# Causal attention of a two-layer model: values projected by pair of head groups instead of by batch element

## Chip, cores and metric

One core of one Trainium2 chip. The metric is the device time of one execution in microseconds; the program before takes 2349.78 us, the median of 3 runs (2348.75 to 2349.86).

## The reference, cut to what matters

Four batch elements of 1024 tokens with 512 channels go through a decoder layer (causal self-attention, cross-attention to 64 context rows, feed-forward) and then a gated fusion. The change touches the causal self-attention alone:

```python
xn1 = _ln(x, g1, be1)
q = einsum('btc,hcd->bhtd', xn1, Wq) + bq      # 16 heads of 32 channels
k = einsum('bsc,hcd->bhsd', xn1, Wk) + bk
v = einsum('bsc,hcd->bhsd', xn1, Wv) + bv
scores = einsum('bhtd,bhsd->bhts', q, k) / scale
scores = where(tril, scores, -inf)
out = einsum('bhts,bhsd->bhtd', softmax(scores), v)
```

## The kernel before

**The stages.** The program has a causal stage (the first 1000 us or so), a cross-attention stage and a feed-forward stage. The first steps of the cross stage (names that begin with "2") are planned into the end of the causal one.

**Groups.** The causal stage works through 16 groups, numbered g: group g is four heads of batch element b = g // 4. Each group has two halves of 512 query tokens (c2 = 0, 1). Half 0 meets 4 key tiles of 128 tokens, half 1 meets 8. For each key tile j and each head i of the group there is a score matmul (step "sc", L785), an exponential on ScalarE ("ex", L895; on diagonal tiles VectorE adds a mask first, "low", L1011), and a product with the values ("pv", L797): the 128x32 slice of the value tile for that head is the stationary operand, the exponentials move, and four heads fill the four column strips of bank 7. POOL adds up the exponentials (L660), and at the end of a half the step "fin" (L806) turns these sums into row sums on TensorE.

**Work for later groups, laid between.** While group g attends, TensorE also does, in the gaps of that order: the query and key projections of a group one or two ahead ("pj", four units for each group, lines 55 to 57), the row maxima of the next group ("mx", L745, reduced on VectorE by L1000 and L1004), the transposes of the next batch element's normalised input ("lnT", L722) in groups 1 and 2 of each batch element, and the value projections ("vm").

**Values before.** A unit of "vm" is one key tile: 128 tokens by all 512 value columns of one batch element, in one PSUM bank. Inputs and weights are split into a high and a low part, so each of the 4 channel tiles k takes three matmuls (the function three, lines 55 to 57): 12 matmuls of 512 moving columns a unit, 8 units for a batch element, 32 in all. ScalarE then copies the bank into Q.v ("ve", L873). Q.v is 128 x 8 x 512 and holds the values of one batch element, all key tiles. So the copy of key tile st for the next batch element has to wait until the last group of this one has used it in "pv". For that reason the eight units of batch element b stand in the last 69% of group 4b-1 and at the start of group 4b; for batch element 0 they stand ahead of group 0. At the very start Q.v also holds the raw input rows of batch element 0 (two of its eight slots for each quarter of the tokens), until they are transposed.

**What sets the order.** order1 gives every step a planned time; the unit is one group (group g runs from g to g + 1, half 1 begins at g + 0.31). at0 turns microseconds of the start-up into that unit: at0(72) is 0. All engines' programs and the queue of SyncE (SP), which issues the DMAs, go through the same list sorted by planned time, each taking its own steps in that order. The units of "vm", "pj" and "mx" are cut into small steps by spread, so that they stand between the score matmuls. banks1 hands the 7 other PSUM banks out ahead of time: each use takes the bank whose last use is planned to end first, and on the chip it waits until that last use has in fact been read. All waits are semaphores with counts known when the program is built.

Of the kernel before, what the change touches and what calls it, by code (L numbers as in the profile page):

```python
# [120 lines left out]

def order1():

    cut = 0.31
# [18 lines left out]
    for b in range(NB):  # L143
        for qt in range(4):
            if b:
                t += ln_times(b, qt, 4 * b - 2.5 if qt == 0 else 4 * b - 2.28 + 0.26 * qt, 4 * b - 2.05 + 0.25 * qt)
        for st in range(8):
            if b == 0:
                s, d = at0(44 + 3.1 * st), 0.05
            else:  # L150
                s, d = 4 * b - 1 + cut + (1 - cut) * (st + 2.2) / 9, 0.057
            t += spread(s, s + d, [(("vm", b, st, k), 1) for k in range(KT)])
            t.append((s + d, ("ve", b, st)))
    for g in range(16):
        if g == 0:
            at = [at0(a) for a in (25, 30, 35, 40)]
        elif g == 1:
            at = (-0.22, -0.13, -0.02, 0.08)
        elif g % 4 == 0:
            at = (g - 1.67, g - 1.5, g - 1.22, g - 1.11)  # L160
        else:
            at = (max(g - 1.87, 0.2), max(g - 1.63, 0.4), g - 1.4, g - 1.2)
        for c2 in range(2):
            for wq in range(2):
                n = 2 * c2 + wq
                t += proj_times(g, c2, wq, at[n], at[n] + (0.05 if g < 2 else 0.07 if g % 4 == 0 else 0.15))
                back = (g - 2 + cut, g - 2 + cut + (1 - cut) * 0.54, g - 1, g - 1)[n] + 0.03
                t.append((at[n] + 0.1 if g == 0 else max(at[n] + 0.22, back), ("stack", g, c2, wq)))
        m0, m1, end = (at0(46), at0(54), cut - 0.12) if g == 0 else (0.25, 0.5, 0.97) if g == 1 else (g - 1.02, g - 0.72, g)
        t += spread(m0, m1, max_steps(g, 0)) + spread(m1, end, max_steps(g, 1))  # L170
        for c2, at in enumerate((m1, end)):
            t += [(at + 0.04, ("mxT", g, c2)), (at + 0.06, ("tq", g, c2)), (at + 0.09, ("tqd", g, c2))]
        for c2 in range(2):
            steps = spread(g + cut * c2, g + (1 if c2 else cut), attn_steps(g, c2))
            t += steps
            for at, s in steps:
                if s[0] == "sc" and s[3] >= 4 * c2:
                    t += [(at + 0.014, ("low", *s[1:])), (at + 0.028, ("ex", *s[1:]))]
                elif s[0] == "sc":
                    t.append((at + 0.001, ("ex", *s[1:])))  # L180
            end = g + (1 if c2 else cut)
# [39 lines left out]

def order2():


    T, X0 = 0.207, 16.68
    E = X0 + 28 * T
    at2 = lambda n: X0 + T * n if n < 28 else E + 0.82 * T * (n - 28)
    t = [(a, s) for a, s in ((14.4, ("2kc",)), (14.66, ("2kb",)), (14.8, ("2wb",)), (14.87, ("2bw",)), (14.6, ("2z", 2)), (15.02, ("2z", 0)),
                             (15.03, ("2z", 1)), (14.9, ("2cd",)))]
    for k in range(KT):  # L230
        t += [(14.02 + 0.1 * k, ("2ld", 0, k)), (14.42 + 0.08 * k, ("2ld", 1, k)), (14.76 + 0.08 * k, ("2ld", 2, k)),
              (14.07 + 0.1 * k, ("2kv", 0, k)), (15.32 + 0.02 * k, ("2kv", 1, k))]
# [1924 lines left out]
```

## Time and profile before

| what | value |
|---|---|
| runs | 2349.86, 2348.75, 2349.78 us; median 2349.78 |
| span of the profiled execution, first to last instruction | 2338.9 us |
| what lies around it, against the median of the runs | 10.9 us |
| instructions | 31417 |
| mean granted TensorE clock | 0.976 |
| TensorE busy (matmuls) | 2198.0 us, 94% |
| VectorE, ScalarE, POOL busy | 60%, 37%, 40% |
| from the first score matmul of group 0 to that of group 14 | 113.3 to 898.7 us |

The profile shows one execution. The profiled execution's own time outside the profiler is not given; its span is 10.9 us below the median of the three runs, and differences are carried over from one to the other. A group's place in the trace is found by counting score matmuls (L785): there are 48 in each group, and the first of them is taken as the group's start. Matmuls are pipelined and the profile models their ends, so a matmul's own duration is longer than its share of the engine's time: what one costs in a run of them is the distance from start to start.

### The profile page before, as it was taken

The page shows a single profiled execution, that of the slowest core. Times are in us where ns is not written, and L with a number is a line of the kernel's source. Part 1 is how long each engine was busy: PE and PEld are TensorE (multiplying, and loading weights), DVE is VectorE, ACT ScalarE, POOL GpSimd, SP SyncE. Part 2 cuts the span into 40 slices and gives each one's busy share as a digit, 9 for nine tenths or more (in the row PEclk, how much of TensorE's full clock was granted, in tenths as well). Part 3 has the DMA queues.
Part 4 walks back from the last instruction along what each step waited for, and adds up shares of the span by engine and source line. Part 5 has one row for each costly group of instructions (what it writes and reads, how often), then busy time and mean ns, then how long its engine had stood idle before and what let it go on. Part 6 is the DMA issues. An engine that isn't in the chain of part 4 may idle for free.

```text
span 2338.9 us, 31417 instructions
## 1 busy us (share of the span) xinstructions
PE 2198.0 (94%) x11206; PEld 1595.5 (68%) x11206; DVE 1410.1 (60%) x3349; ACT 868.2 (37%) x1598; POOL 933.6 (40%) x943
## 2 busy tenths in 40 slices
PE   7999999999999998789999998999999999999996
PEld 5655565556555654447777776788887887888784
DVE  5477757875786566735666668453455546454646
ACT  3155545654565455533443334321111122112213
POOL 1068657766777577773333333010111202011212
PEclk9999999999999998789999999999999999999998
DMA  7465545553556356212111121321112121212011
GB/s 231 55 93 97 92 71 77 103 93 62 83 97 97 60 88 124 69 56 85 59 55 55 59 95 55 113 86 36 50 54 75 52 82 44 87 55 68 33 36 50
DMA packets 106320, 177.29 MB, mean 76 GB/s; under 512 B 18334, under 2 KB 23454, under 8 KB 106160
## 3 DMA queue, kind: packets, MB, share of 16 engines
q1 hardware_dynamic: 106164, 175.29, 32.4%
q8 instruction: 88, 1.44, 0.3%
q14 instruction: 68, 0.56, 0.1%
HBM read 83.67 MB, written 40.13 MB: 53 GB/s over the span
## 4 chain that ended last, share of the span: by engine, by line
PE 75%; DVE 9%; issue 6%; ACT 4%; POOL 3%; DMA 2%; SPq 0%; POOLq 0%; ACTq 0%; DVEq 0%
PE psum L55 18%; PE psum L56 17%; PE psum L57 17%; PE psum L797 5%; PE psum L745 5%; PE psum L785 4%; PE psum L806 2%; DMA small<-es 2%; PE psum L703 1%; DVE psum L1000 1%; POOL es L660 1%; ACT sx L1346 1%; PE psum L1300 1%; DVE mx L1004 1%; PE psum L1292 1%
## 5 line engine op out<-in xcount | busy, mean ns | idle before, releaser
L660 POOL TENSOR_TENSOR es<-es,er 128x512 f32<-128x512 f32 (+3 forms) x640 | 589.6, 961 | 322.5 <-PE psum L797 283.4
L895 ACT ACTIVATE er<-psum 128x512 f32<-128x512 f32 (+3 forms) x640 | 280.4, 470 | 316.0 <-DVE psum L1011 181.2
L1000 DVE CUSTOM_DVE_ANT_0 psum<-psum,mask_ts 128x384 f32<-128x384 f32 (+3 forms) x512 | 247.9, 500 | 201.2 <-PE psum L745 200.5
L785 PE MATMUL psum<-qs,ks 100*128 100x512 f32 (+3 forms) x768 | 264.5, 377 | 17.1 <-DVE mx L1004 6.6
L745 PE MATMUL psum<-ks,qs 96*128 96x512 f32 (+3 forms) x768 | 267.2, 373 | 10.9 <-DVE mx L1000 6.6
L1850 ACT ACTIVATE fy<-psum,cols 128x512 f32<-128x512 f32 x128 | 88.2, 689 | 451.4 <-PE psum L57 450.9
L745 PEld LDWEIGHTS psum<-ks,qs 96*128 96x128 f32 x768 | 144.0, 194 | 109.7 <-issue 39.4
L1004 DVE TENSOR_REDUCE mx<-psum 128x1 fp32r<-128x512 f32 x256 | 175.1, 684 | 60.7 <-PE psum L745 59.8
L785 PEld LDWEIGHTS psum<-qs,ks 100*128 100x128 f32 x768 | 145.9, 196 | 92.4 <-DVE mx L1004 23.1
L55 PE MATMUL psum<-fh,hh 128*128 128x512 f32 x512 | 201.1, 393 | 7.1 <-DVE hl L1951 7.1
L55 PE MATMUL psum<-fah,fh 128*128 128x512 f32 x512 | 202.6, 396 | 0.0
L57 PE MATMUL psum<-fah,fl 128*128 128x512 f32 x512 | 199.8, 390 | 0.0
L56 PE MATMUL psum<-fal,fh 128*128 128x512 f32 x512 | 199.6, 390 | 0.0
L57 PE MATMUL psum<-fh,hl 128*128 128x512 f32 x512 | 199.4, 389 | 0.0
L56 PE MATMUL psum<-fl,hh 128*128 128x512 f32 x512 | 199.3, 389 | 0.0
L1949 DVE CAST hh<-fy 128x512 fp32r<-128x512 f32 x128 | 59.5, 465 | 228.8 <-ACT fy L1850 228.4
L1215 POOL TENSOR_TENSOR pp<-pp,small 128x1024 f32<-128x1024 f32 x32 | 61.2, 1913 | 266.7 <-DVE small L1481 266.7
L797 PE MATMUL psum<-er,v 128*32 128x512 f32 (+3 forms) x1280 | 152.3, 497 | 6.7 <-ACT er L895 6.2
L1746 POOL TENSOR_TENSOR et<-et,vpb 128x512 f32<-128x512 f32 x24 | 35.4, 1476 | 284.8 <-ACT et L1876 284.8
L1011 DVE TENSOR_TENSOR psum<-psum,mask_st 128x128 f32<-128x128 f32 x512 | 138.3, 303 | 15.0 <-PE psum L785 14.1
L55 PEld LDWEIGHTS psum<-fh,hh 128*128 128x128 f32 x512 | 96.1, 188 | 29.0 <-DVE hl L1951 9.5
L57 PEld LDWEIGHTS psum<-fah,fl 128*128 128x128 f32 x512 | 96.2, 188 | 20.5
(258 smaller groups left out, 4479.8 us busy)
## 6 DMA issues: line engine op xcount, KB each, us to landing
qs<-stage SPq DMA_DIRECT2D x96, 256.0 KB, 5.7
ks<-stage SPq DMA_DIRECT2D x96, 256.0 KB, 6.9
rs<-rs_d SPq DMA_DIRECT2D x32, 256.0 KB
sa_d<-rs SPq DMA_DIRECT2D x32, 256.0 KB, 2.2
sx<-sa_d SPq DMA_DIRECT2D x8, 1024.0 KB, 5.7
xt<-in_x SPq DMA_DIRECT2D x32, 256.0 KB, 6.1
x_d<-xt SPq DMA_DIRECT2D x32, 256.0 KB, 2.0
fw<-in_Wf SPq DMA_DIRECT2D x16, 512.0 KB, 5.3
```

The lines of the kernel that those rows point to most:

```text
L55: e.matmul(dst, lh, rh, start=start, stop=False)
L56: e.matmul(dst, lh, rl, start=False, stop=False)
L57: return e.matmul(dst, ll, rh, start=False, stop=stop)
L660: e.tensor_tensor(es, es, er, ALU.add).then_inc(s_add.sem, 1)
L745: t = e.matmul(bank1(*s)[:, v * wd:v * wd + wd], Q.qs[par][0:96, i, 128 * ti:128 * ti + 128], Q.ks[par][0:96, i, c0:c0 + wd], start=True, ...
L785: t = e.matmul(ps[:, off:512], Q.ks[par][0:100, i, 128 * j:128 * j + 128], Q.qs[par][0:100, i, 512 * c2 + off:512 * c2 + 512], start=True, ...
L797: e.matmul(bank[BO][32 * i:32 * i + 32, off:512], Q.v[:, j, h:h + 32], src[:, off:512], start=j == 0, stop=j == nj - 1).then_inc(s_pv.sem, 1)
L895: e.activation(dst, bank1("sc", g, c2, j, i)[:, off:512], ACT.Exp, scale=SCALE).then_inc(s_freeS.sem, 1)
L1000: t = e.tensor_tensor_reduce(out=ps, in0=ps, in1=mask_ts[:, 512 - wd:512], scale=1.0, scalar=-3e38, op0=ALU.add, op1=ALU.max, accum_out=mx ...
L1004: e.tensor_reduce(mx[:, at:at + 1], bank1(*s)[:, 0:wd], AX, ALU.max).then_inc(s_red.sem, 1)
L1011: e.tensor_tensor(ps, ps, mask_st[:], ALU.add).then_inc(s_low.sem, 1)
L1850: e.activation(y[:], ring3(("h", c, m)), ACT.Relu, bias=col("bf1", m), scale=1.0).then_inc(s_r3.sem, 1)
```

## The change

Values are projected for a pair of groups (q = g // 2: eight heads, 256 columns) instead of for all sixteen heads of a batch element. A unit of "vm" is now two key tiles (sp: tiles 2sp and 2sp + 1) by 256 columns, the two key tiles in the two halves of one bank: 2 x 4 channel tiles x 3 matmuls, that is 24 matmuls of 256 moving columns. There are 4 units for a pair, 8 for a batch element, 32 in all. Q.v keeps its size; the pairs take its two halves in turn, and a pair's copy waits for the pair two before it. The planned times change with it: the units of pair q stand in 4 places from 1.4 or 1.2 groups ahead of the pair's first group. The other times become named constants with the same values, but for two small shifts: the projections of group 2 (0.13 and 0.37 instead of 0.2 and 0.4) and the restacking DMAs ("stack") of groups 4, 8 and 12 (at most 0.08 earlier).

```diff
+LN_LOAD = (-2.5, -2.02, -1.76, -1.5)
+LN_TURN = (-2.05, -1.8, -1.55, -1.3)
+CUT = (0.31, 0.31, 0.31, 0.31)
+PROJ_0 = (25, 30, 35, 40)
+PROJ_1 = (-1.22, -1.13, -1.02, -0.92)
+PROJ = ((-1.67, -1.5, -1.22, -1.11), (-1.87, -1.63, -1.4, -1.2), (-1.87, -1.63, -1.4, -1.2), (-1.87, -1.63, -1.4, -1.2))
+PROJ_LONG = (0.07, 0.15, 0.15, 0.15)
+VALUES_0 = (48, 54, 60, 66)
+VALUES = ((-1.2, -0.95, -0.7, -0.45), (-1.4, -1.1, -0.8, -0.5))
+VALUES_LONG = 0.1
 def order1():
-        for st in range(8):
-            if b == 0:
-                s, d = at0(44 + 3.1 * st), 0.05
-            else:
-                s, d = 4 * b - 1 + cut + (1 - cut) * (st + 2.2) / 9, 0.057
-            t += spread(s, s + d, [(("vm", b, st, k), 1) for k in range(KT)])
-            t.append((s + d, ("ve", b, st)))
     for g in range(16):
-            at = (max(g - 1.87, 0.2), max(g - 1.63, 0.4), g - 1.4, g - 1.2)
+        r = g % 4
+        at = [at0(a) for a in PROJ_0] if g == 0 else [g + a for a in (PROJ_1 if g == 1 else PROJ[r])]
-                t.append((at[n] + 0.1 if g == 0 else max(at[n] + 0.22, back), ("stack", g, c2, wq)))
+                t.append((at[n] + 0.1 if g == 0 else max(at[n] + PROJ_LONG[r] + 0.07, back), ("stack", g, c2, wq)))
+        if g % 2 == 0:
+            for sp in range(4):
+                s, d = (at0(VALUES_0[sp]), 0.05) if g == 0 else (g + VALUES[r // 2][sp], VALUES_LONG)
+                t += spread(s, s + d, [(("vm", g // 2, sp, i), 1) for i in range(4)])
+                t.append((s + d, ("ve", g // 2, sp)))
+        def values(g):
+
+            return Q.v[:, 4 * (g // 2 % 2):4 * (g // 2 % 2) + 4, :].rearrange("p a (s n) -> p (a s) n", n=256)
 def pe1(e, w):
                 elif s[0] == "vm":
-                    _, b, st, k = s
-                    if k == 0:
+                    _, q, sp, i = s
+                    b, half = divmod(q, 2)
+                    st = 2 * sp + i // 2
+                    if i == 0:
                         free1(w, *s[:3])
                     w.wait_ge(s_wl1, 12)
-                    xn_ready(w, b, st // 2, k)
-                    ss = slice(128 * st, 128 * st + 128)
+                    ss, cs, to = slice(128 * st, 128 * st + 128), slice(256 * half, 256 * half + 256), slice(256 * (i // 2), 256 * (i // 2) + 256)
                     Wh, Wl = Q.W["v"]
-                    t = three(e, bank1(*s[:3]), (Q.xh[:, k, ss], Q.xl[:, k, ss]), (Wh[:, k, :], Wl[:, k, :]), k == 0, k == 3)
-                    if k == 3:
+                    for k in range(2 * (i % 2), 2 * (i % 2) + 2):
+                        xn_ready(w, b, st // 2, k)
+                        t = three(e, bank1(*s[:3])[:, to], (Q.xh[:, k, ss], Q.xl[:, k, ss]), (Wh[:, k, cs], Wl[:, k, cs]), k == 0, k == 3)
+                    if i == 3:
                         t.then_inc(s_fillA.sem, 1)
...
-                        w.wait_ge(s_v, 8 * (g // 4) + j + 1)
+                        w.wait_ge(s_v, 4 * (g // 2) + j // 2 + 1)
...
-                        h = 128 * gg + 32 * i
-                        e.matmul(bank[BO][32 * i:32 * i + 32, off:512], Q.v[:, j, h:h + 32], src[:, off:512],
+                        h = 128 * (g % 2) + 32 * i
+                        e.matmul(bank[BO][32 * i:32 * i + 32, off:512], values(g)[:, j, h:h + 32], src[:, off:512],
 def act1(e, w):
                 elif s[0] == "ve":
-                    if b:
-                        w.wait_ge(s_pv, Q.pv[4 * b - 1, 1, st, 3] + 1)
-                    e.activation(Q.v[:, st, :], bank1("vm", b, st), ACT.Copy).then_inc(s_v.sem, 1)
+                    if q >= 2:
+                        w.wait_ge(s_pv, Q.pv[2 * q - 3, 1, 2 * sp + 1, 3] + 1)
+                    else:
+                        w.wait_ge(s_fillA, Q.useA["lnT", 0, 2 * q + sp // 2, 1] + 1)
+                    e.activation(values(2 * q)[:, 2 * sp:2 * sp + 2, :], bank1("vm", q, sp).rearrange("p (s n) -> p s n", n=256),
+                                 ACT.Copy).then_inc(s_v.sem, 1)
```

## Rows read from the trace of the kernel before

**Rows 1.** The page: span, busy time of TensorE, granted clock in 40 slices.

```profile
span 2338.9 us, 31417 instructions
...
PE 2198.0 (94%) x11206; PEld 1595.5 (68%) x11206; DVE 1410.1 (60%) x3349; ACT 868.2 (37%) x1598; POOL 933.6 (40%) x943
...
PEclk9999999999999998789999999999999999999998
```

**Rows 2.** Busy time by stretch, one stretch a group: window, width, engines' busy (instructions), clock.

```profile
72.00:113.30 41.30, 41.30 (x188) 29.31 (x188) 18.45 (x51) 7.13 (x13) 0.00 (x0) 1.00 0.17 23
113.30:167.50 54.20, 52.57 (x290) 32.62 (x288) 43.72 (x142) 27.62 (x58) 37.19 (x40) 1.00 0.62 91
167.50:218.80 51.30, 48.81 (x274) 28.61 (x273) 38.67 (x126) 28.90 (x61) 36.81 (x40) 0.97 0.55 83
218.80:276.70 57.90, 52.24 (x291) 30.91 (x289) 44.65 (x146) 35.32 (x71) 40.46 (x47) 0.97 0.53 102
276.70:344.00 67.30, 66.00 (x349) 43.29 (x348) 37.19 (x126) 31.05 (x65) 44.31 (x51) 1.00 0.48 77
344.00:394.10 50.10, 48.80 (x281) 29.78 (x277) 35.85 (x123) 28.14 (x60) 34.10 (x34) 1.00 0.47 70
394.10:446.10 52.00, 48.42 (x274) 28.68 (x273) 38.74 (x123) 29.04 (x61) 40.33 (x46) 1.00 0.59 93
446.10:503.10 57.00, 52.31 (x290) 30.92 (x288) 43.82 (x144) 35.28 (x71) 41.20 (x49) 0.97 0.54 104
...
620.50:673.90 53.40, 51.46 (x274) 30.73 (x273) 38.74 (x120) 28.93 (x61) 40.35 (x46) 0.90 0.58 91
673.90:731.40 57.50, 53.12 (x290) 31.08 (x288) 44.68 (x146) 35.28 (x71) 41.10 (x48) 0.94 0.54 103
...
848.90:898.70 49.80, 47.33 (x265) 27.87 (x265) 35.59 (x122) 27.31 (x58) 38.96 (x43) 1.00 0.56 87
898.70:965.40 66.70, 54.49 (x246) 29.80 (x245) 49.76 (x126) 29.05 (x62) 47.12 (x52) 0.75 0.55 128
```

**Rows 3.** Instructions of the value weights' high part, in group 3, then group 4.

```profile
L55 PE MATMUL psum<-wvh,xh x28: 389/397/504, 302.0 to 342.8; 128*128 128x512 f32 x28
```

```profile
L55 PE MATMUL psum<-wvh,xh x4: 395/395/442, 344.6 to 348.0; 128*128 128x512 f32 x4
```

**Rows 4.** TensorE in order of time: start, duration (us), line; value matmuls.

```profile
102.59 0.40 PE L55 MATMUL psum<-wvh,xh 128*128 128x512 f32 x1
...
103.29 0.40 PE L55 MATMUL psum<-wvh,xh 128*128 128x512 f32 x1
```

**Rows 5.** Groups by line and shape: busy us, mean ns; the transposes of input rows.

```profile
L722 PE MATMUL psum<-ident,xr 128*128 128x128 f32 x96 | 16.5, 297 | 7.3 <-ACT xr L837 5.0 <-DVE mx L1000 1.3 <-ACT er L895 0.9
```

**Rows 6.** The view of rows 4 in the cross stage: split matmuls of 256 columns.

```profile
1061.91 0.28 PE L55 MATMUL psum<-kbh,qh 128*128 128x256 f32 x1
...
1062.86 0.28 PE L57 MATMUL psum<-kbh,ql 128*128 128x256 f32 x1
```

**Rows 7.** TensorE in order of time, idle before and releaser: groups 5, 6, 8, 9.

```profile
397.89 2.19 PE L806 MATMUL psum<-es,sm 128*32 128x512 f32 x8 [0.84 <-POOL es L660]
...
433.51 0.44 PE L785 MATMUL psum<-qs,ks 100*128 100x384 f32 x1 [1.22 <-DVE mx L1004]
...
449.50 0.44 PE L785 MATMUL psum<-qs,ks 100*128 100x384 f32 x1 [0.49 <-DVE mx L1000]
...
484.09 0.88 PE L722 MATMUL psum<-ident,xr 128*128 128x128 f32 x4 [1.67 <-ACT xr L837]
...
620.20 0.41 PE L797 MATMUL psum<-er,v 128*32 128x128 f32 x2 [0.55 <-ACT er L895]
...
661.31 0.45 PE L785 MATMUL psum<-qs,ks 100*128 100x384 f32 x1 [1.72 <-DVE mx L1004]
```

**Rows 8.** ScalarE's copies of values out of PSUM: duration min/median/max, first and last start.

```profile
L873 ACT ACTIVATE v<-psum x32: 592/598/604, 66.3 to 803.7; 128x512 f32<-128x512 f32 x32
...
  PE psum L57: 54.5, 23
```

More of the change, by code:

```diff
@@ L119, in attn_steps @@
     yield ("none",), 200
+LN_LOAD = (-2.5, -2.02, -1.76, -1.5)
[8 more added lines that the diff above has]
+VALUES_LONG = 0.1
+MAX_0 = 0.19
+MAX_1 = (-0.75, -0.5, -0.03)
+MAX = ((-1.02, -0.72, 0.0), (-1.02, -0.72, 0.0), (-1.02, -0.72, 0.0), (-1.02, -0.72, 0.0))
 def order1():
-    cut = 0.31
     at0 = lambda us: (us - 72) / 58
@@ L142, in order1 @@
             t.append((at0(at + 4), ("zo", u)))
-    for b in range(NB):
+    for b in range(1, NB):
         for qt in range(4):
-            if b:
-                t += ln_times(b, qt, 4 * b - 2.5 if qt == 0 else 4 * b - 2.28 + 0.26 * qt, 4 * b - 2.05 + 0.25 * qt)
-        for st in range(8):
-            if b == 0:
-                s, d = at0(44 + 3.1 * st), 0.05
-            else:
-                s, d = 4 * b - 1 + cut + (1 - cut) * (st + 2.2) / 9, 0.057
-            t += spread(s, s + d, [(("vm", b, st, k), 1) for k in range(KT)])
-            t.append((s + d, ("ve", b, st)))
-    for g in range(16):
[L155 to L161, printed above, removed]
-            at = (max(g - 1.87, 0.2), max(g - 1.63, 0.4), g - 1.4, g - 1.2)
+            t += ln_times(b, qt, 4 * b + LN_LOAD[qt], 4 * b + LN_TURN[qt])
+    for g in range(16):
+        r = g % 4
+        cut = CUT[r]
+        at = [at0(a) for a in PROJ_0] if g == 0 else [g + a for a in (PROJ_1 if g == 1 else PROJ[r])]
         for c2 in range(2):
@@ L165, in order1 @@
                 n = 2 * c2 + wq
-                t += proj_times(g, c2, wq, at[n], at[n] + (0.05 if g < 2 else 0.07 if g % 4 == 0 else 0.15))
-                back = (g - 2 + cut, g - 2 + cut + (1 - cut) * 0.54, g - 1, g - 1)[n] + 0.03
-                t.append((at[n] + 0.1 if g == 0 else max(at[n] + 0.22, back), ("stack", g, c2, wq)))
-        m0, m1, end = (at0(46), at0(54), cut - 0.12) if g == 0 else (0.25, 0.5, 0.97) if g == 1 else (g - 1.02, g - 0.72, g)
+                t += proj_times(g, c2, wq, at[n], at[n] + (0.05 if g < 2 else PROJ_LONG[r]))
@@ new lines, in order1 @@
+                back = g - 2 + (CUT[(g - 2) % 4] if n == 0 else CUT[(g - 2) % 4] + (1 - CUT[(g - 2) % 4]) * 0.54 if n == 1 else 1) + 0.03
+                t.append((at[n] + 0.1 if g == 0 else max(at[n] + PROJ_LONG[r] + 0.07, back), ("stack", g, c2, wq)))
[4 more added lines that the diff above has]
+                t.append((s + d, ("ve", g // 2, sp)))
@@ L170, in order1 @@
+        m0, m1, end = (at0(46), at0(54), MAX_0) if g == 0 else [g + a for a in (MAX_1 if g == 1 else MAX[r])]
         t += spread(m0, m1, max_steps(g, 0)) + spread(m1, end, max_steps(g, 1))
-        for c2, at in enumerate((m1, end)):
-            t += [(at + 0.04, ("mxT", g, c2)), (at + 0.06, ("tq", g, c2)), (at + 0.09, ("tqd", g, c2))]
+        for c2, a in enumerate((m1, end)):
+            t += [(a + 0.04, ("mxT", g, c2)), (a + 0.06, ("tq", g, c2)), (a + 0.09, ("tqd", g, c2))]
         for c2 in range(2):
-            steps = spread(g + cut * c2, g + (1 if c2 else cut), attn_steps(g, c2))
+            end = g + (1 if c2 else cut)
+            steps = spread(g + cut * c2, end, attn_steps(g, c2))
@@ L175, in order1 @@
             t += steps
-            for at, s in steps:
-                if s[0] == "sc" and s[3] >= 4 * c2:
-                    t += [(at + 0.014, ("low", *s[1:])), (at + 0.028, ("ex", *s[1:]))]
+            for a, s in steps:
+                if s[0] == "sc" and s[3] >= 4 * c2 :
+                    t += [(a + 0.014, ("low", *s[1:])), (a + 0.028, ("ex", *s[1:]))]
                 elif s[0] == "sc":
-                    t.append((at + 0.001, ("ex", *s[1:])))
-            end = g + (1 if c2 else cut)
+                    t.append((a + 0.001, ("ex", *s[1:])))
@@ L240, in order2 @@
         if c == 0:
-            ld, sp, w1, step, ln = 15.78, 15.86, 15.9, 0.07, 16.22
+            (ld, sp, w1, ln), step = CROSS_0, 0.07
         else:
@@ L484, in released @@
             elif use[0] == "vm":
-                w.wait_ge(s_v, 8 * use[1] + use[2] + 1)
+                w.wait_ge(s_v, 4 * use[1] + use[2] + 1)
             elif use[0] == "pj":
```

30 lines of the change are left out of this document (17 added, 13 removed).

## The prediction

> **What bounds the kernel.** The page comes first: TensorE is busy for 94% of the span, the others for 60% or less, and the clock it was granted is near full almost everywhere [rows 1]. The change lies in the causal stage, so the stage has to be read by itself, one group a stretch [rows 2]. Three things are to be seen. Width less PE busy is TensorE's idle time: 1.3 us in groups 3 and 4 (67.30 less 66.00, 50.10 less 48.80), but 2.5, 3.6, 1.9 and 2.5 in groups 1, 5, 9 and 13, and 5.7, 4.7 and 4.4 in groups 2, 6 and 10. In these the granted clock is also below 1: down to 0.90 in group 9, where a tenth of full clock over 53.4 us means 10.7 us at the lower level, 1.2 GHz. And no other engine is full anywhere. So groups with value units are bound by TensorE; the others wait a little for one another.
>
> How far each is from TensorE's own bound follows from groups 3 and 4. Group 3 holds 28 of the first matmuls of value steps, group 4 holds 4 [rows 3]; four make a unit, so 7 units and 1. Three value matmuls of 512 columns go from 102.59 to 103.29 [rows 4], 0.233 us each, so a unit of 12 costs 2.80. Without them group 3 is 67.3 - 19.6 = 47.7 and group 4 is 50.1 - 2.8 = 47.3: the bare group. Groups 1, 5, 9 hold 2 sets of four transposes and groups 2, 6, 10 six; 24 sets are busy for 16.5 us [rows 5], 0.69 each, of which the modelled tail of a last matmul is 0.17 (0.40 drawn, 0.233 spent [rows 4]): some 0.5 a set. That makes bounds of 48.3 and 50.4. Against them the slack is 3.0, 3.7 and 5.1 in groups 1, 5 and 9, 2.5 in group 13 (bare), and 7.5, 6.6 and 7.1 in groups 2, 6 and 10 [rows 2].
>
> **Part 1, matmuls of half the width.** 384 matmuls of 512 columns become 768 of 256, with twice the weight loads. The nearest rows are the cross stage's split matmuls of 256 columns, each with its own 128x128 weights: eight steps in 1062.86 - 1061.91 = 0.95 us, 0.119 each [rows 6]. A unit is 24 x 0.119 = 2.85 against 2.80: +0.05 x 32 = **+1.8 us**. Below nothing it can't be, since no column is dropped; the upper end, every extra load exposed, is a rival below. A rule of the Trainium skill speaks for that end: "TensorE: Matmul & The Clock Gate", Part 3 (Packing small matmuls), says that a weight load overlaps matmuls under way only when its row group differs, and these loads all take the whole array; its 107 ns for a load of 128 columns, an estimate from that page, would add about 41 us. The trace doesn't agree: full-array loads and 256-column matmuls alternate at 0.119 us [rows 6].
>
> **Part 2, ahead of group 0.** From 72 us to the first score TensorE is busy for all 41.3 us while VectorE does 18.5 and ScalarE 7.1 [rows 2]. Four of the eight units leave (4 x 2.80 = 11.2 us) and nothing else is near its limit, so the first score comes at about 102 instead of 113.3. The four come back as pair 1, planned at 0.6, 0.9, 1.2 and 1.5: two in group 0, two in group 1. Group 0 is 54.2 wide with 1.6 idle and takes them at full price: 59.9. Alone this is worth nothing.
>
> **Part 3, levelling.** For batch elements 1 to 3, eight units stood in groups 3 and 4 (7 and 1), and likewise later. Now the pair that begins at g = 4 has its units at 2.8, 3.05, 3.3 and 3.55, the next at 4.6, 4.9, 5.2 and 5.5. Group 2 gets 1, group 3 keeps 3, groups 4 and 5 get 2 each. In the groups with slack a unit should cost less than 2.85, because TensorE was waiting there anyway. The waits are in rows 7: row sums wait for POOL just after group 5's start (0.84, and about as much again, by my estimate, inside the burst drawn out to 2.19), the last value products of group 8 wait for exponentials (0.55), scores wait for a bank that VectorE has yet to reduce at three quarters of groups 5 and 9 (1.22, 1.72). All belong to engines that run behind a TensorE that is too fast; a unit ahead of each gives them 2.85 us. The units at 4.6 and 4.9 stand ahead of the POOL wait, those at 5.2 and 5.5 ahead of the bank wait. The slack of groups 1, 5, 9 and 13 is 3.0 + 3.7 + 5.1 + 2.5 = 14.3 us. The ends are 0 and 14.3; I take 65%, since row sums and final products should be covered in full, the bank waits in part (the new units hold a bank themselves for a tenth of a group, 5 us, against 3.3): **-9.3 us**, with the drops in clock that follow such waits.
>
> Groups 2, 6 and 10 have the most slack and get little of it. Their waits are in the first third (0.49) and at the transposes (1.67, for ScalarE's normalising) [rows 7], and the one unit stands behind both, at 0.8. Between 0 and -2.9 each I take -0.4: **-1.2 us**.
>
> **Part 4, what is uncovered.** Value steps ran across the boundaries into groups 4, 8 and 12, and there TensorE did not wait. Now the last unit ends at 3.65. What is late next is what the boundary into group 6 shows: short waits for exponentials and for a bank, 0.49 the longest [rows 7], about 1 us a boundary: 3 x 1.0 = **+3.0 us**. The low end is 0, the high end the boundary into group 5, some 2.0 us by the estimate above, with a drop in clock.
>
> **Part 5, at nothing.** ScalarE makes as many copies (32 of 0.598 us [rows 8]); 54.5 us of its waits before them were for value matmuls [rows 8], and ScalarE is only half busy. Spread out, a copy stands in front of exponentials in other groups, 0.6 us each; uncovered, 0.6 x 16 moved copies would be 9.6 us, but seven banks buffer scores, so I keep 0. The copies' old wait for the products of the same key tile goes; the new waits (the pair two before, or transposes long done) were met a group earlier, so nothing queues behind them on ScalarE. SP issues the same DMAs; the restacks of groups 4, 8 and 12 move 4 us forward at most past other loads, and their matmuls come later than that. Group 2's projections move by 0.07 groups at most. POOL's steps stay. Groups 14 and 15 [rows 2], where VectorE and DMAs for the cross stage bound, keep their work.
>
> **The sum.** 1.8 + 0 - 9.3 - 1.2 + 3.0 = -5.7 us. Against the span of 2338.9 that gives 2333.2, and with the 10.9 us around it, against the median of the runs of 2349.8, **2344.1 us**. A measurement of this kernel tells about 0.2%, 4.7 us, from no change.
>
> **Rivals.**
> - **The slack is filled whole** (20%): groups 1, 5, 9, 13 reach their bound (-14.3), the boundaries stay covered by projections and maxima, and the clock stays at 2.4 GHz: 1.8 - 14.3 = -12.5, 2337.3 us. For it: the waits in rows 7 are each shorter than one unit. Against it: a bank is a shared thing.
> - **Moved, not filled** (20%): TensorE's waits are a fixed lag between a score and its release, and reappear behind the new units. Then only +1.8 and a little either way: 2351 us, no change. For it: groups 0 and 4, with value work, still idle 1.6 and 1.3 us.
> - **Slower, at the starts of groups 4, 8 and 12** (15%): POOL did 44.3 us of work in group 3's 67.3; in the new 56 us it is 79% full, as in group 5's 52 (78%), which is where TensorE ran into it. Each boundary then costs 2.0 us and a stretch at 1.2 GHz as in group 1, where 0.97 over 51.3 us lost 1.5: 3 x 3.5 + 1.8 = 12.3; with only a third of the slack won (-4.8) it is +7.5, 2357.3. It decides once less than 12.3 us of slack is won.
> - **The loads are exposed** (3%): 0.188 us for each of the loads as the profile draws them, instead of 0.119, is 0.069 x 768 = +53, some 2400 us. Rows 6 speak against it.
> - **Nothing of the prologue comes back** (2%): the first score stays at 113 for a cause not seen on the engines' rows; +11, 2355.
>
> The forecast itself has 40%, and of it three fifths lie under 2345.1. Faster by over 0.2%: 0.24 + 0.20 = 0.44. Within: 0.15 of the forecast, 0.18 of the moved, 0.04 of the slower side, 0.37. Slower: the rest, 0.19. The range runs from the full filling with a little beyond, 2336, to the slower rival, 2357; outside lie the exposed loads and the tails. The likeliest case's own range is 2340 to 2350.
>
> **What would show it.** 11590 matmuls instead of 11206, the value ones 128x256 and 0.119 apart. First score near 102 us. Group widths near 60, 54.5, 60, 56 for 0 to 3, then 54, 55, 59.5, 56 for 4 to 7, and 54 for 12 and 13; the start of group 14 near 893 instead of 898.7. No wait for POOL just after group 5 begins, a shorter one for L1004 at its three quarters. Groups 14 and later as before, shifted. I am wrong if group 3 is 56 but groups 4 and 5 add up to over 111 (nothing absorbed), if group 4 begins with a wait for POOL near 0.8, or if 256-column matmuls stand over 0.13 apart.

## The result, and the profile after

The changed kernel takes 2329.51 us (median of 4 runs, 2324.11 to 2332.26) against 2349.27 before; the ratio on record is 0.9927 with a 95% interval of 0.9912 to 0.9942, 17 us in 2349 and some 14 to 21 us by the interval. The two medians alone are 19.8 us apart (0.9916), the two profiled spans 16.6; where this text adds up parts it goes by the ratio. Forecast were 2344.1 us and a range of 2336 to 2357. The direction was right, the size a third of it, and the range missed it.

The page of the changed kernel, the same three lines as [rows 1]:

```profile
span 2322.3 us, 32170 instructions
...
PE 2180.8 (94%) x11590; PEld 1608.7 (69%) x11590; DVE 1410.7 (61%) x3349; ACT 863.9 (37%) x1598; POOL 933.7 (40%) x943
...
PEclk9999999999999999789999999999999999999998
```

11590 matmuls, as forecast. TensorE is busy for 94% again: the share tells nothing of the 16.6 us by which the span is shorter (2338.9 to 2322.3). The stretches do. This is the busy time by group of the changed kernel; the columns are those of [rows 2], which it answers to (ahead of group 0, groups 0 to 7, 9, 10, 12, 13 and 14):

```profile
72.00:102.40 30.40, 30.40 (x173) 21.96 (x172) 15.71 (x43) 5.00 (x9) 0.00 (x0) 1.00 0.22 30
102.40:162.20 59.80, 57.96 (x338) 38.52 (x337) 44.13 (x144) 28.88 (x60) 37.89 (x41) 1.00 0.57 83
162.20:216.70 54.50, 52.23 (x325) 33.59 (x321) 38.81 (x125) 29.88 (x63) 37.30 (x40) 1.00 0.52 78
216.70:279.50 62.80, 55.61 (x315) 34.22 (x313) 43.88 (x145) 35.41 (x72) 42.08 (x49) 0.95 0.52 100
279.50:334.00 54.50, 53.97 (x340) 36.25 (x337) 36.43 (x122) 28.76 (x61) 38.05 (x42) 1.00 0.49 74
334.00:386.60 52.60, 51.55 (x313) 33.17 (x313) 36.12 (x121) 28.14 (x60) 41.53 (x47) 1.00 0.56 93
386.60:441.00 54.40, 52.36 (x325) 33.63 (x321) 38.92 (x126) 29.77 (x63) 38.12 (x42) 1.00 0.52 78
441.00:502.60 61.60, 55.28 (x316) 33.85 (x313) 44.02 (x145) 35.50 (x72) 41.34 (x48) 0.94 0.52 98
502.60:556.90 54.30, 53.85 (x337) 36.18 (x336) 36.23 (x120) 28.75 (x61) 38.79 (x43) 1.00 0.51 78
...
609.50:664.30 54.80, 52.39 (x325) 33.56 (x321) 39.25 (x127) 29.76 (x63) 38.14 (x42) 1.00 0.52 78
664.30:726.50 62.20, 55.56 (x315) 34.33 (x313) 44.07 (x145) 35.41 (x72) 42.30 (x50) 0.95 0.51 102
...
781.00:833.60 52.60, 51.56 (x314) 33.18 (x313) 36.14 (x121) 28.14 (x60) 41.59 (x47) 1.00 0.57 94
833.60:885.40 51.80, 50.93 (x317) 32.93 (x313) 35.38 (x119) 28.01 (x60) 36.59 (x39) 1.00 0.49 73
885.40:949.60 64.20, 51.12 (x246) 27.70 (x245) 51.85 (x133) 28.89 (x62) 45.75 (x50) 0.81 0.56 132
```

Two things are to be seen. Group 14 starts at 885.4 instead of 898.7: 13.3 of the 16.6 us are won ahead of it. And groups 2, 6 and 10 got 4.9, 4.6 and 4.7 us wider for one unit of 2.85 us, with the granted clock at 0.94 or 0.95: something was lost there too.

The price of a value matmul was as forecast. These lines show the changed kernel's TensorE in order of time (start, duration), and answer to [rows 4, 6]: five steps in 0.59 us, 0.118 each.

```profile
281.85 0.28 PE L56 MATMUL psum<-wvl,xh 128*128 128x256 f32 x1
...
282.44 0.40 PE L805 MATMUL psum<-qs,ks 100*128 100x512 f32 x1
```

Part of the widening of group 2 starts on VectorE. Its instructions in order of time in the changed kernel, with the idle time before them: it waits 2.34 us for input rows to come from memory. The same wait stands in groups 6 and 10 (2.35 and 2.29 us), and in none of the three in the kernel before.

```profile
251.86 0.69 DVE L988 BATCH_NORM_STATS2 small<-xr 128x6 f32<-128x512 f32 x1 [2.34 <-DMA xr<-in_x]
```

Behind it on VectorE are maxima whose banks TensorE wants. TensorE in order of time, same kernel, just after: 2.0 us of waits that the kernel before does not have there, and then the old one for the transposes, as in [rows 7].

```profile
253.21 0.50 PE L762 MATMUL psum<-ks,qs 96*128 96x512 f32 x1 [1.40 <-DVE mx L1023]
...
254.55 0.44 PE L762 MATMUL psum<-ks,qs 96*128 96x384 f32 x1 [0.60 <-DVE mx L1027]
...
258.06 1.09 PE L739 MATMUL psum<-ident,xr 128*128 128x128 f32 x4 [1.68 <-ACT xr L857]
```

Why the rows are late stands in SP's queue. The DMA issues of the changed kernel in that stretch (start, duration, line): the restacking of group 4's queries goes first, and the input rows behind it.

```profile
243.07 1.91 SPq L599 DMA_DIRECT2D qs<-stage  x3
245.02 1.10 SPq L589 DMA_DIRECT2D xr<-in_x  x2
```

In the kernel before the rows went first:

```profile
246.40 0.81 SPq L572 DMA_DIRECT2D xr<-in_x  x2
247.30 1.91 SPq L582 DMA_DIRECT2D qs<-stage  x3
```

Behind the restacking the rows also take longer to arrive. These lines give KB and the median us from issue to landing, first for the changed kernel (242 to 253 us), then for the kernel before (242 to 254 us):

```profile
xr<-in_x SPq DMA_DIRECT2D x2, 256.0 KB, 6.8
...
xr<-in_x SPq DMA_DIRECT2D x2, 256.0 KB, 3.0
```

One word on the base: the changed kernel's profiled run of 2324.11 us has a span of 2322.3, 1.8 us less. The 10.9 us that the front of this document puts around the span before were for the most part not around it: that profiled execution was one of the faster ones.

### The profile page after: what moved, and what is told of

The parts are those of the page before. It is cut to its first block, busy times and chain, and to the rows that moved or that the text cites. A ratio compares the mean times of both kernels' runs of the same rounds, so it can differ in the third digit from the quotient of the medians.

```text
span 2322.3 us, 32170 instructions
## 1 busy us (share of the span) xinstructions
PE 2180.8 (94%) x11590; PEld 1608.7 (69%) x11590; DVE 1410.7 (61%) x3349; ACT 863.9 (37%) x1598; POOL 933.7 (40%) x943
## 4 chain that ended last, share of the span: by engine, by line
PE 76%; DVE 10%; ACT 5%; issue 3%; DMA 2%; POOL 2%; SPq 1%; POOLq 0%; DVEq 0%; ACTq 0%
PE psum L55 18%; PE psum L56 17%; PE psum L57 17%; PE psum L817 5%; PE psum L762 5%; PE psum L805 4%; DVE psum L1023 2%; PE psum L720 1%; ACT sx L1369 1%; PE psum L826 1%; DMA small<-es 1%; DMA xr<-in_x 1%; DVE mx L1027 1%; DVE stage L1009 1%; ACT es L918 1%
## 5 line engine op out<-in xcount | busy, mean ns | idle before, releaser
L817 PE MATMUL psum<-er,v 128*32 128x512 f32 (+3 forms) x1280 | 143.5, 493 | 0.4 <-ACT er L918 0.2
```

What stands on the lines that cost most here:

```text
L817: e.matmul(bank[BO][32 * i:32 * i + 32, off:512], values(g)[:, j, h:h + 32], src[:, off:512], start=j == 0, stop=j == nj - 1).then_inc(s_p ...
```

## Experiments

Each kernel ran on one chip beside runs of the kernel before; ratios are against those. The base drifts with the chip (medians 2345.1 to 2349.3), so kernels are compared by ratio, times 2349 us. "First sixth" of a group is the stretch of its first 8 score matmuls.

**1. Narrow units at the old places.**

```diff
-                s, d = (at0(VALUES_0[sp]), 0.05) if g == 0 else (g + VALUES[r // 2][sp], VALUES_LONG)
+                b, st = g // 4, 4 * (r // 2) + sp
+                s, d = (at0(44 + 3.1 * st), 0.05) if b == 0 else (4 * b - 1 + cut + (1 - cut) * (st + 2.2) / 9, 0.057)
```

> The changed kernel with its narrow units (two key tiles by 256 columns) put back at the eight planned places that the value units had before: 8 ahead of group 0, 7 and 1 in groups 3 and 4, and likewise later. If the gain comes from where the units stand (theory), this is the kernel before plus the price of narrower matmuls: +1.8 us by 0.119 against 0.233 us, 2346 to 2353 us, group 3 about 67.5 us wide. If the gain comes from the units themselves (the split of the bank, the copies' other waits), it keeps most of it: 2328 to 2336 us, and group 3 is 65 us or less.

Measured: 2355.6 us, ratio 1.0029 (1.0017 to 1.0041), group 3 67.9 us wide. The whole gain, and more, comes from where the units stand. But the ratio stands for 6.8 us, 5 us beyond the forecast price of narrow matmuls, so something else in the change costs.

**2. Pair 1 back ahead of group 0.**

```diff
-                s, d = (at0(VALUES_0[sp]), 0.05) if g == 0 else (g + VALUES[r // 2][sp], VALUES_LONG)
+                s, d = (at0(44 + 3.1 * (2 * g + sp)), 0.05) if g <= 2 else (g + VALUES[r // 2][sp], VALUES_LONG)
```

> The changed kernel with the four units of pair 1 back ahead of group 0, at the places of before; the rest as changed. If moving them into groups 0 and 1 won only what group 1 had idle, the first score returns to about 113.5 us, group 0 falls by 5.7 to 54, group 1 by 3 to 4 to about 51, and the whole is 2 to 3 us slower than the changed kernel. If the prologue was where time was won, it is 5 us slower or more.

Measured: 2331.63 us, ratio 0.9930 (0.9910 to 0.9951), against 0.9927 with the move. First score at 113.6, group 0 54.4 wide, group 1 51.3. The move takes 11.2 us off the prologue and gives 5.3 and 3.2 to groups 0 and 1, some 2.7 us by widths, less than the runs can tell.

**3. No unit in groups 2, 6 and 10.**

```diff
-VALUES = ((-1.2, -0.95, -0.7, -0.45), (-1.4, -1.1, -0.8, -0.5))
+VALUES = ((-0.95, -0.72, -0.5, -0.28), (-1.4, -1.1, -0.8, -0.5))
```

> The changed kernel with the four units of the pairs that begin at groups 4, 8 and 12 planned at 0.95, 0.72, 0.5 and 0.28 ahead instead of 1.2, 0.95, 0.7 and 0.45: all four in group 3 (7, 11), none in group 2 (6, 10), which the change made 4.6 to 4.9 us wider for a unit of 2.85. If the unit there is what makes TensorE wait for VectorE, groups 2, 6 and 10 fall back to 57 to 58 us, group 3 rises by 2.85 to 57.3, and the whole is 4 to 6 us faster than the changed kernel. If the extra wait comes from the other fillers' new banks and not from this unit, groups 2, 6, 10 fall by 2.85 at most and the time stays within 2 us.

Measured: 2332.01 us, ratio 0.9928 (0.9911 to 0.9944), the same as the changed kernel. Groups 2, 6 and 10 fell by 2.1, 0.3 and 1.3, groups 3, 7 and 11 rose from 54.4 to 57.4, by 3.0. So the unit is not what widened group 2 by 4.9 us: it accounts for 0.3 to 2.1 us in these three groups.

**4. A third of the value matmuls.** The low parts of the value projection are left out.

```diff
-                        t = three(e, bank1(*s[:3])[:, to], (Q.xh[:, k, ss], Q.xl[:, k, ss]), (Wh[:, k, cs], Wl[:, k, cs]), k == 0, k == 3)
+                        t = e.matmul(bank1(*s[:3])[:, to], Q.xh[:, k, ss], Wh[:, k, cs], start=k == 0, stop=k == 3)
```

> The changed kernel with one of the three matmuls of each value step (high times high alone), so a unit is 8 matmuls and 0.95 us instead of 24 and 2.85; the low parts of the value projection are left out. If TensorE now has no slack where units stand, every group falls by 1.9 us a unit: groups 3, 7, 11 by 5.7, groups 0, 1, 4, 5, 8, 9, 12, 13 by 3.8, groups 2, 6, 10 by 1.9, in all 60.8 us. Where a group falls by less, the missing work was hidden in waits: the theory says groups 1, 5, 9 and 13 fall by 1 to 2 us only, the others in full, some 50 us in all.

Measured: one run, with nothing to tell its scatter from, 2301.51 us, 28 us under the changed kernel's median (span 2299.7, 22.6 under), where 50 were expected and 60.8 us of matmuls were left out. Busy time by group of this kernel, groups 3, 4, 5 and 13:

```profile
270.44:321.60 51.16, 50.30 (x290) 31.12 (x289) 36.05 (x121) 28.65 (x61) 39.03 (x43) 1.00 0.55 85
321.60:371.68 50.08, 48.69 (x281) 29.79 (x280) 35.20 (x120) 28.14 (x60) 39.22 (x43) 1.00 0.56 87
371.68:428.44 56.76, 53.02 (x292) 31.78 (x289) 41.05 (x127) 29.92 (x63) 44.21 (x53) 0.94 0.54 86
...
807.22:857.55 50.33, 49.01 (x284) 29.80 (x281) 36.17 (x121) 28.23 (x60) 38.79 (x43) 1.00 0.55 86
```

Groups 4 and 13 stop at 50.1 and 50.3 us. Group 5 even widened from 54.4 to 56.8, with the clock at 0.94; since group 9 takes 57.7 us at 0.94 in experiment 2 with its units whole, this one execution doesn't show that the missing work is the cause. About 50 us is what a group takes whether it holds no unit ([rows 2], group 13: 49.8), a third of two (here), or one ([rows 2], group 4: 50.1).

**5. The restacking DMAs at their old times.**

```diff
-                t.append((at[n] + 0.1 if g == 0 else max(at[n] + PROJ_LONG[r] + 0.07, back), ("stack", g, c2, wq)))
+                t.append((at[n] + 0.1 if g == 0 else max(at[n] + 0.22, back), ("stack", g, c2, wq)))
```

> The changed kernel with the restacking DMAs (stack) of groups 4, 8 and 12 at their old planned times. The change put them at 2.47 instead of 2.55, ahead of the load of the last input rows (planned at 2.50) on SP's queue; in the changed kernel's trace VectorE waits 2.34 us for these rows in group 2 with maxima behind it, and TensorE waits for their banks. Theory: the order on SP's queue is the cause of the wider groups 2, 6 and 10 (62.8, 61.6, 62.2 us), which fall to 59 to 60, and the whole is 5 to 9 us faster than the changed kernel (2329.5): 2321 to 2325. Rival: the groups are wide because of the value unit at 0.8 or the banks; then the time stays within 2 us.

Measured: 2319.85 us, ratio 0.9894 (0.9876 to 0.9913) against 0.9927: 7.8 us faster than the changed kernel, some 2 to 13 by the two intervals. Groups 6 and 10 of this kernel answer to 61.6 and 62.2:

```profile
440.22:498.54 58.32, 55.04 (x316) 33.55 (x314) 44.17 (x145) 35.41 (x72) 39.72 (x46) 0.94 0.55 101
660.75:720.17 59.42, 55.40 (x315) 33.93 (x313) 43.87 (x145) 35.36 (x72) 41.11 (x48) 0.94 0.53 100
```

Group 2 fell only to 62.2 in this execution; the wait for the rows is gone there too, but the clock is 0.95 again and other waits on VectorE and on a restacking DMA were longer. In experiment 13, with the same old times, it is 60.3.

**6. Narrow units alone**: experiment 1 with the edit of experiment 5.

> Narrow value units at the eight old places, and the restacking DMAs at their old times too: the width of the units and the layout of the values alone. Theory: +1.8 us against the kernel before (ratio 1.0008), 2349 to 2352, and groups 2, 6, 10 as wide as before. If the narrow units cost more than their start-to-start times say, it stays near the 2355.6 of the kernel with narrow units and moved DMAs.

Measured: 2351.36 us, ratio 1.0022 (1.0013 to 1.0032), 12 runs: +5.2 us, between the two expectations. Groups 3 and 11 are 67.9 wide against 67.3, so seven units show 0.5 us, 32 some 2 us, as forecast. The other 3 us have no sure place in the rows. This kernel also keeps the change's earlier projections of group 2, so it is not quite the narrow units alone: the first sixth of group 0 has one projection step more and takes 11.0 us against 10.3, but group 0 in all is only 0.2 wider. And the profiled execution has lower clock in groups 5, 7 and 9. The cause stays open, and the earlier projections were never run by themselves.

**7. The kernel before again.**

> The kernel before once more, for a second profile: its first profiled execution had a span of 2338.9 us, 10 us under the median of the runs. Theory: that execution was at the fast end of what drops of TensorE's clock allow; this one has a span of 2343 to 2349 us with the difference in groups 2, 6, 10 and from 14 on, and groups 3, 4, 5, 7, 8, 11, 12, 13 within 0.3 us of 67.3, 50.1, 52.0, 67.3, 50.1, 67.3, 50.1, 49.8. If the profile has an offset of 10 us of its own, all groups are the same again.

Measured: 2342.05 us with a span of 2340.2. Groups 4, 8, 12 and 13 are 50.1, 50.1, 50.0 and 49.8 again; groups 3 and 7 are 68.0 and 68.1 where the clock dropped, group 2 59.4. The groups that kept full clock and hold no transposes repeat to 0.1 us, and the scatter of the whole (2339 to 2357 over all runs of the kernel before) comes from the others. The offset of 10.9 us is refuted: 1.8.

**8. The kernel before with early restacking DMAs alone.**

```diff
-                t.append((at[n] + 0.1 if g == 0 else max(at[n] + 0.22, back), ("stack", g, c2, wq)))
+                t.append((at[n] + 0.1 if g == 0 else max(at[n] + (0.14 if g % 4 == 0 else 0.22), back), ("stack", g, c2, wq)))
```

> The kernel before with the restacking DMAs of groups 4, 8 and 12 at the changed kernel's planned times and nothing else. Theory (order on SP's queue): 4 to 8 us slower than the kernel before, 2353 to 2357, groups 2, 6 and 10 wider by 2 us or more, and VectorE waiting about 2 us for input rows in each. Rival (units or banks): no change.

Measured: 2357.24 us, ratio 1.0042 (1.0027 to 1.0057), +9.9 us. Groups 2, 6 and 10 of this kernel, against 57.9, 57.0 and 57.5 [rows 2] (59.4, 57.0 and 57.5 in experiment 7):

```profile
219.99:280.85 60.86, 55.44 (x292) 32.24 (x290) 44.88 (x146) 35.22 (x71) 39.14 (x46) 0.89 0.51 97
453.66:513.73 60.07, 53.10 (x291) 31.40 (x289) 44.22 (x145) 35.11 (x71) 37.98 (x43) 0.94 0.53 98
684.38:744.39 60.01, 54.47 (x291) 31.84 (x290) 44.15 (x145) 35.12 (x71) 41.23 (x49) 0.91 0.53 99
```

And its waits in group 2 (engine and line, whom it waited for, total, times, longest), the same one:

```profile
DVE small L965 <- DMA xr<-in_x: 2.3, 1, 2.3
```

Two DMA issues that changed places on SP's queue, in an edit of 0.08 in a planned time, cost some 8 us in the changed kernel and 10 in the one before, each give or take several us. Between experiments 1 and 6 the same edit makes 1.2, 1.8 and 2.6 us in groups 2, 6 and 10, but only 0.0007 in the ratio, 1.6 us, within the intervals. So the wait is the same everywhere, and what it costs in all is not the same number each time. This was in the change and is no part of what it is about.

**9 and 10. Row sums asked for later**, in the kernel before (9) and in the kernel of experiment 5 (10).

```diff
-            t += [(end + 0.02, ("sao", g, c2)), (end + 0.08, ("fin", 2 * g + c2))]
-            t += [(end + a, (s, 2 * g + c2)) for a, s in ((0.14, "f0"), (0.26, "f1"), (0.3, "f1d"), (0.42, "f2"), (0.62, "f3"), (0.69, "f3d"))]
+            t += [(end + 0.02, ("sao", g, c2)), (end + 0.14, ("fin", 2 * g + c2))]
+            t += [(end + a, (s, 2 * g + c2)) for a, s in ((0.2, "f0"), (0.26, "f1"), (0.3, "f1d"), (0.42, "f2"), (0.62, "f3"), (0.69, "f3d"))]
```

> The kernel before with the row sums (fin) planned 0.14 instead of 0.08 after a half's end and their DMA (f0) 0.20 instead of 0.14 after it; value units untouched. Theory: spreading the value units won most of its time at the starts of groups, where row sums wait for POOL's last additions (idle and a drawn burst, about 2 us in groups 3, 5, 7, 9, 11, 13), and not in bank waits in the middle. Then asking for the row sums 3 us later wins it too, without moving a unit: first sixth of group 5 down from 9.6 to about 8 us, the whole 8 to 12 us faster than before. Rival (the gain is TensorE's idle time filled by units, wherever it is): 3 us or less.

> The changed kernel with the restacking DMAs at their old times and the row sums planned 0.14 after a half's end. Theory: the units at 0.05 and 0.1 around the groups' starts already gave POOL the time it needs, so little is left, 0 to 3 us faster than the same without the late row sums (2319.85), 2316 to 2320. Rival (two gains that add up): 8 us or more faster, under 2312.

Measured: 9: 2348.37 us, ratio 1.0006 (0.9996 to 1.0016), nothing won. 10: 2335.79 us, ratio 0.9959 (0.9944 to 0.9974), 15 us lost against experiment 5. The theories of both fell; for 9 the rival holds by its number (3 us or less), for 10 neither side does. The first sixth of group 3 tells one reason; width, TensorE busy and, third from the end, the granted clock. The kernel before:

```profile
276.66:286.25 9.59, 8.52 (x42) 4.49 (x42) 5.85 (x33) 5.64 (x11) 5.29 (x10) 1.00 0.91 139
```

With late row sums:

```profile
277.52:287.09 9.57, 9.57 (x41) 6.63 (x41) 6.59 (x33) 5.01 (x10) 6.36 (x11) 0.66 0.93 141
```

The idle 1.07 us went to nothing, and the clock from 1.00 to 0.66, that is for two thirds of the stretch at 1.2 GHz. The width is the same to 0.02 us.

But that is one group. In groups 7 and 13 of the same execution the clock stayed at 1.00, and there the first sixth did fall, from 9.57 and 9.56 to 8.53 and 8.33 us:

```profile
506.71:515.24 8.53, 7.83 (x41) 4.10 (x41) 6.45 (x34) 4.81 (x10) 6.47 (x11) 1.00 0.89 143
854.11:862.44 8.33, 7.71 (x42) 4.05 (x42) 5.92 (x29) 4.82 (x10) 6.48 (x11) 1.00 0.89 142
```

In groups 5, 9 and 11 it is 9.9, 9.8 and 10.1 at 0.83. So later row sums win 1.0 to 1.2 us at a start where the clock holds. Drops to such a clock there are found in the kernel before too (group 9: 10.4 us at 0.67; groups 3 and 7 in experiment 7: 10.3 and 10.4), so experiment 9 doesn't show that the edit caused them. In experiment 10 it is plainer: all six first sixths of groups 4, 5, 8, 9, 12 and 13 have a clock of 0.83 or 0.84 and are 1.9 to 2.1 us longer, and none has in experiment 5. Those of groups 4 and 5 were 8.4 and 7.8 us at 1.00 in experiment 5; in experiment 10, group 5:

```profile
388.74:398.67 9.93, 9.21 (x44) 4.56 (x41) 6.42 (x33) 4.82 (x10) 2.27 (x4) 0.83 1.05 124
```

**11. One unit moved to the start of groups 3, 7 and 11**, in the kernel of experiment 6.

```diff
-                s, d = (at0(44 + 3.1 * st), 0.05) if b == 0 else (4 * b - 1 + cut + (1 - cut) * (st + 2.2) / 9, 0.057)
+                s, d = (at0(44 + 3.1 * st), 0.05) if b == 0 else (4 * b - 0.95, 0.1) if st == 0 else (4 * b - 1 + cut + (1 - cut) * (st + 2.2) / 9, 0.057)
```

> Narrow units at the old places with old restacking times (2351.36 us before), and one unit of each batch element moved: from the middle of groups 3, 7 and 11 to 0.05 behind their start. Row sums asked for later did not win time: idle before them went (1.1 to 0.0 us in group 3's first sixth) but the granted clock of that sixth fell to 0.7, 9.6 us both times. New theory: at a group's start TensorE has too little to do, and pays either by idling or at the lower clock; only work laid there is carried free. Then this one move wins about 2 us a start: group 3's first sixth is 10.3 (7.5 without the unit), groups 3, 7 and 11 fall from 67.9 to 65.8, the whole by 6 us to 2345. Rival (price is the same wherever a unit stands, the gain of the change comes from elsewhere): no change.

Measured: 2344.18 us, ratio 0.9990 (0.9976 to 1.0005) against 1.0022: 7.5 us faster than experiment 6, and the two intervals don't meet. Groups 3, 7 and 11 of this kernel, with the same seven units:

```profile
278.69:345.13 66.44, 66.22 (x434) 49.28 (x433) 37.67 (x127) 30.83 (x65) 44.33 (x51) 0.97 0.49 78
505.07:571.16 66.09, 65.83 (x433) 48.18 (x432) 37.67 (x127) 30.85 (x65) 44.35 (x51) 1.00 0.49 78
734.48:800.60 66.12, 65.89 (x433) 48.27 (x433) 37.48 (x127) 30.86 (x65) 44.34 (x51) 1.00 0.49 78
```

67.9, 68.7 and 67.9 were these in experiment 6. The first sixth of group 11 is 10.7 us with the unit and 9.6 without: a unit of 2.85 us at this start costs about 1.

**12 and 13. Projections over the starts**, in the kernel before (12) and in that of experiment 5 (13).

```diff
-            at = (g - 1.67, g - 1.5, g - 1.22, g - 1.11)
+            at = (g - 1.67, g - 1.5, g - 1.22, g - 1.04)
         else:
-            at = (max(g - 1.87, 0.2), max(g - 1.63, 0.4), g - 1.4, g - 1.2)
+            at = (max(g - 1.87, 0.2), max(g - 1.63, 0.4), g - 1.4, g - (1.2 if g % 4 == 3 else 1.08))
```

```diff
-PROJ = ((-1.67, -1.5, -1.22, -1.11), (-1.87, -1.63, -1.4, -1.2), (-1.87, -1.63, -1.4, -1.2), (-1.87, -1.63, -1.4, -1.2))
+PROJ = ((-1.67, -1.5, -1.22, -1.11), (-1.87, -1.63, -1.4, -1.08), (-1.87, -1.63, -1.4, -1.2), (-1.87, -1.63, -1.4, -1.2))
```

> The kernel before, value units untouched, with the last projection of the next groups moved over the starts of groups: planned 1.08 ahead instead of 1.2 for groups 4b+1 and 4b+2 (over the starts of 4b and 4b+1), 1.04 instead of 1.11 for groups 4, 8, 12 (over the starts of 3, 7, 11). New theory (work of any kind over the start): first sixths of groups 3, 5, 7, 9, 11, 13 fall from 9.6 to about 7.8 net of it, 6 to 12 us faster than before, 2334 to 2340. Rival (value units matter, not any work): no gain, or slower because the restacked projections come late.

> The changed kernel with restacking DMAs at their old times (2319.85) and the last projection of groups 5, 9 and 13 over the starts of groups 4, 8 and 12, where the first sixth is 8.4 us against 7.5 in group 3. New theory: about 1 us a start, 2 to 3 us faster, 2316 to 2318. Rival: nothing, within 1 us.

Measured: 12: 2345.84 us, ratio 0.9990 (0.9977 to 1.0002), at most 5 us where 6 to 12 were expected; groups 3, 7 and 11 fell by 1.0 to 1.7, groups 4, 8 and 12 rose by 1.5. 13: 2318.17 us, ratio 0.9877 (0.9859 to 0.9894); against experiment 5 (0.9894) that is within the intervals. The rows say more than the totals. In experiment 12 the first sixths of groups 3, 5, 7, 9 and 13 hold three projection matmuls more (0.70 us) and are yet 0.6 to 0.8 us narrower than 9.6, at full clock, group 7 for one:

```profile
509.84:518.63 8.79, 8.57 (x44) 4.82 (x43) 5.75 (x24) 5.61 (x11) 4.49 (x9) 1.00 0.92 149
```

So projection work at these starts is carried too. But the first sixths of groups 4, 8 and 12, where a value unit stood already, rose by 0.8, the full price, and groups 1, 5 and 9 had a clock of 0.94. That it makes the whole kernel faster is not shown.

The fastest measured are experiments 13 and 5, 1.2% and 1.1% under the kernel before, both faster than the kernel before and the changed one.

## Why the prediction was wrong

By ratios, the change comes apart like this: narrow units, with the earlier projections of group 2, **+5.2 us** (experiment 6), spreading them **-30** (experiment 5 against 6), early restacking DMAs **+7.8** (changed kernel against experiment 5), in all -17. Forecast were +1.8, -7.5 (-9.3 - 1.2 + 3.0) and 0. The first part has some 2 us of scatter by the intervals, the second 5, the third 6, and the split depends on the order: by way of experiment 1, with the DMAs early on both sides, spreading is worth 24 us and not 30.

- **The bound was read wrongly, and this is the step that failed.** The prediction took groups 3 and 4 as bound by TensorE, subtracted 7 and 1 units at 2.80 each and called the rest, 47.7 and 47.3, the bare group. The rows it stood on said otherwise: group 13 without a unit and group 4 with one are 49.8 and 50.1 wide [rows 2]. The first unit was free already. The profiles together give a group without transposes (4, 13, 3) by the units it holds: 49.8 with none, 50.1 with one, 51.8 to 52.6 with two, 54.4 with three, 57.4 with four (experiment 3), 67.9 with seven (experiment 6). The next unit costs 0.3, about 2, about 2, 3.0, and then 3.5 each. Three units in 54.4 leave 45.9, so the bare group was 1.4 to 1.8 us less than forecast, and there was slack in every group, groups 3 and 4 among them. Taking four units from group 3 won 13.5 us (experiment 6 to 5) and not 11.2; giving one to group 4 cost 2.5 and two to group 13 cost 1.9. This list mixes the number of units with their place. The one unit of group 4 stands at its start (first sixth 9.8 us against 9.6 in group 13 without it); and with one of the seven moved to the start the group takes 66.1 (experiment 11), which makes 2.9 each beyond four, full price.
- **What that is in the sum.** Groups 3, 7 and 11 fell by 12.9 us each where the forecast had 11.1, and groups 4, 8 and 12 rose by 2.5 where it had 3.9: together 9.7 us. The term of -9.3 was too small as well. Groups 1, 5, 9 and 13 took eight units, 22.8 us, for 9.1 us of width, so 13.7 us were absorbed (12.9 against the execution of experiment 7) where 65% of 14.3 was forecast. By its size that is the rival of the slack filled whole. Against that, groups 2, 6 and 10 rose by 14.1 where 7.4 was forecast.
- **A reading of the rows.** The prediction says of groups 1, 5, 9, 13, 2, 6 and 10 that their clock was below 1. [Rows 2] has 1.00 for groups 5 and 13; the sum doesn't use it.
- **Idle time was read as width less busy.** Group 3 showed 1.3 us so. But its first sixth took 9.6 us, and net of the unit that stands there now it takes 7.5 (10.3 less 2.8, experiment 5). A waiting burst is drawn as busy: eight row-sum matmuls took 2.19 us in [rows 7] and take 1.06 in the changed kernel (group 5, in order of time), where the idle before is 0.38 and POOL no longer ends it:

```profile
389.30 0.44 PE L805 MATMUL psum<-qs,ks 100*128 100x384 f32 x1 [0.38 <-ACT es L918]
389.68 1.06 PE L826 MATMUL psum<-es,sm 128*32 128x512 f32 x8
```

- **The slower rival** had the place right, the starts of groups 4, 8 and 12, and the size wrong: their first sixth is 8.4 us against 7.0 net before, 1.4 each, near the 1.0 of part 4. Its cause is not what is seen. POOL did 38.1 us of work in group 3's 54.5 (70%, where the rival had 79%) and 41.5 in group 4, so part of its work lies behind that start now; but the row sums there take 1.07 us, and TensorE doesn't wait for POOL.
- **The mid-group waits stayed.** The bank wait at three quarters of group 5, 1.22 us in [rows 7], is 1.01 in the changed kernel:

```profile
429.19 0.44 PE L805 MATMUL psum<-qs,ks 100*128 100x384 f32 x1 [1.01 <-DVE mx L1027]
```

What was won lies at starts and ends. Group 13 shows it by sixths (8 score matmuls each), less 2.85 us for each unit: the first falls from 9.6 to 7.8, the second from 6.9 to 6.3, the last from 7.5 to 6.1, and the other three stay. No unit stands in that first sixth: the one planned at 12.9 stands at the end of group 12, the next is planned at 13.2. That a unit ahead of the row sums covers their wait for POOL was thus right.
- **The restacking DMAs at nothing** (part 5) was wrong by some 8 us. The prediction did look at SP's queue, and said that the restacks move 4 us forward "past other loads". It did not ask who waits for those loads: the last input rows are needed by statistics on VectorE, which takes its steps in order, with maxima behind them, and TensorE waits for the maxima's banks.
- **What held:** 0.118 us a matmul, so the rival of exposed loads is out; the prologue (102.4 us against 102); groups 0 and 1 at 59.7 and 54.5 (59.9 and 54.5). The Trainium skill's "TensorE: Matmul & The Clock Gate", Part 3 (Packing small matmuls), has a weight load overlap the matmuls under way only when its row group differs. These runs don't agree: each value matmul of the changed kernel has its own load for the whole array, and still they start 0.118 us apart. Of groups 2, 6 and 10 the forecast unit price of 2.45 came out as 1.3 and 1.9 in groups 6 and 10 once the DMAs were back (58.3 and 59.4 against 57.0 and 57.5), and as 1.8 and 1.0 in experiment 13 (58.8 and 58.5); group 2 scatters too much to tell.

What makes a start cheap to fill is shown in part. The wait for POOL is 1.0 to 1.2 us of it, where the clock holds (experiment 9, groups 7 and 13). Where it doesn't, the same time or more goes at 1.2 GHz. A value unit at the start is carried for about 1 us (experiment 11), one at the end of the group before takes 1.8 off the next first sixth (groups 5 and 13), and three projection matmuls there are carried as well (experiment 12). The reading that fits these is that TensorE has too little work around a start and pays by waiting or by the clock. That the little work is what lowers the clock is argued, not shown.

## What to carry to other kernels

Don't subtract work at full price from a busy stretch and call the rest a bound: look for two stretches that differ only by that work, for their difference is its price there. Where the price of one more piece rises with those already in a stretch, spreading them pays even though no work goes away. And when steps in a planned order move, even by little, list which steps they overtake on each queue and follow who waits for the overtaken one through to the engine that bounds.

## What the runs showed of the hardware

A wait removed can come back as clock. In the first sixth of group 3, 1.07 us idle at full clock and no idle at a granted clock of 0.66 took 9.59 and 9.57 us. It need not: with the same edit groups 7 and 13 kept full clock and took 8.53 and 8.33 us. With the units of the changed kernel it came back each time: in group 5, 7.80 us at 1.00 became 9.93 at 0.83 when the row sums moved by 3 us, with hardly more idle (0.43 and 0.72), and groups 4, 8, 9, 12 and 13 went the same way. In that group 5 the clock was at 1.2 GHz from 393.3 to 396.8 us; in the 4.56 us from the group's start to there TensorE had been busy for 3.84.

The order on a DMA queue shows in the time to landing. The same two loads of 256 KB landed 3.0 to 3.6 us after their issue in the kernel before, where they went ahead of the three restacking DMAs, and 6.8 us after it in the changed kernel, where they went behind them (groups 2, 6 and 10; medians of the two).
